# Splitting the value weights of time mixing on GpSimd in the stage before

## What is computed

```python
xn = _layernorm(x, ln_w, ln_b)
prev = jnp.pad(xn[:, :-1, :], ((0, 0), (1, 0), (0, 0)))
xk = xn * tmk + prev * (1.0 - tmk)        # the same for xv (tmv) and xr (tmr)
k = jnp.einsum('btd,ed->bte', xk, Wk)
v = jnp.einsum('btd,ed->bte', xv, Wv)
r = jax.nn.sigmoid(jnp.einsum('btd,ed->bte', xr, Wr))
decay = jax.nn.sigmoid(decay_w)
# over time t: S = decay * S + k_t * v_t, kept for each t as S_seq
out = x + r * jnp.einsum('btd,ed->bte', S_seq, Wo)
```

## Time and profile before

| | us |
|---|---|
| median of 3 runs | 2179.92 |
| lowest and highest | 2178.80, 2180.19 |
| the profiled execution: its time | 2187.31 |
| the profiled execution: its span | 2185.3 |
| busy in the span: TensorE | 2126.6 |
| ScalarE | 1399.6 |
| VectorE | 1391.0 |
| GpSimd | 304.9 |
| the two stages meet at about | 1936 |
| time mixing ends at about | 1994 |

### The profile page before, as it was taken

The page is one execution under the profiler, slowest core; times in us unless marked ns, Lnnn a source line. Parts: engine busy times, 40 slices in busy tenths (PEclk is TensorE's granted clock), DMA queues, the critical chain, the costliest instruction groups (busy, mean ns, idle before and its releaser), DMA issues. The chain is left out here.

```text
span 2185.3 us, 38691 instructions
## 1 busy us (share of the span) xinstructions
PE 2126.6 (97%) x15099; PEld 1654.0 (76%) x15099; DVE 1391.0 (64%) x2369; ACT 1399.6 (64%) x2701; POOL 304.9 (14%) x277
## 2 busy tenths in 40 slices
PE   8999999999999999899999999999999999998998
PEld 6787777787775567688888857777787778777775
DVE  6555455455565753699999974554554554587887
ACT  3666566666655544788888845665666666557774
POOL 1221212112110000200000211211122121103001
PEclk9999999999999999999999999999999999999999
DMA  4001001010104102799999930101000010013996
GB/s 164 20 21 40 21 21 40 21 40 21 34 26 151 36 4 100 307 368 375 356 350 360 364 124 7 39 21 40 21 36 24 21 40 20 21 59 136 362 357 234
DMA packets 53796, 262.10 MB, mean 120 GB/s; under 512 B 9576, under 2 KB 9960, under 8 KB 26992
## 3 DMA queue, kind: packets, MB, share of 16 engines
q1 hardware_dynamic: 47312, 244.42, 30.2%
q0 software_dynamic: 2560, 8.39, 1.1%
q10 hardware_dynamic: 3744, 6.82, 0.8%
HBM read 243.61 MB, written 15.99 MB: 119 GB/s over the span
## 5 line engine op out<-in xcount | busy, mean ns | idle before, releaser
L645 DVE COPY c_pt<-bank 128x512 f32<-128x512 f32 x256 | 177.2, 692 | 560.8 <-PE bank L443 560.7
L863 ACT ACTIVATE c_pr<-wide,c_nmax 128x512 f32<-128x512 f32 x512 | 348.8, 697 | 120.0 <-DVE c_nmax L637 62.1
L443 PE MATMUL bank<-ident,c_pr 128*128 128x128 f32 x2048 | 266.0, 273 | 1.0 <-ACT c_pt L870 0.7
L443 PEld LDWEIGHTS bank<-ident,c_pr 128*128 128x128 f32 x2048 | 238.2, 140 | 37.5 <-DVE c_pt L645 2.1
L841 ACT ACTIVATE c_khi<-bank,c_cols 128x512 fp32r<-128x512 f32 x128 | 87.9, 687 | 252.3 <-PE bank L95 252.3
L870 ACT COPY c_pt<-bank 128x512 f32<-128x512 f32 x256 | 150.4, 587 | 62.0 <-PE bank L443 61.8
L637 DVE CUSTOM_DVE_ANT_0 wide<-wide,land 128x512 f32<-128x512 f32 x256 | 169.2, 723 | 1.9 <-PE wide L427 1.7
L640 DVE TENSOR_REDUCE c_nmax<-wide 128x1 f32<-128x512 f32 x256 | 158.9, 683 | 1.8 <-PE wide L427 1.7
L312 POOL TENSOR_TENSOR c_clo<-land,c_chi 128x512 fp32r<-128x512 f32 x64 | 82.1, 1288 | 510.5 <-ACT c_chi L827 510.5
L459 PEld LDWEIGHTS bank<-c_pt,c_v 128*32 128x32 f32 x4096 | 104.1, 109 | 49.6 <-issue 47.1
L459 PE MATMUL bank<-c_pt,c_v 128*32 128x128 f32 x4096 | 138.4, 276 | 1.5 <-issue 1.4
(11 more groups left out here) (473 smaller groups left out, 5079.8 us busy)
## 6 DMA issues: line engine op xcount, KB each, us to landing
moe_hr<-in_L_ffn_w SPq DMA_DIRECT2D x68, 1024.0 KB, 7.8
land<-in_L_ffn_w SPq DMA_DIRECT2D x34, 1024.0 KB, 8.2
land<-in_ctx SPq DMA_DIRECT2D x31, 1024.0 KB, 4.9
moe_raw<-in_L_ffn_w SPq DMA_DIRECT2D x18, 1024.0 KB, 7.4
moe_raw<-in_L_ffn_we_gate SPq DMA_DIRECT2D x8, 1024.0 KB, 7.8
land<-in_L_ffn_we_up SPq DMA_DIRECT2D x8, 1024.0 KB, 6.9
moe_raw<-in_L_ffn_we_down SPq DMA_DIRECT2D x8, 1024.0 KB, 8.0
moe_raw<-in_L_ffn_we_up SPq DMA_DIRECT2D x7, 1024.0 KB, 7.2
```

Of the source, the lines that this page charges most:

```text
L443: last = pe.transpose(TB[n % 2][:, h * P:(h + 1) * P], pr[:, u % 2, h, n * P:(n + 1) * P], k["ident"][:])
L645: nc.vector.tensor_copy(pt[:, n, :], TB[0][:]).then_inc(pt_dve, 1)
L863: nc.scalar.activation(pr[:, u % 2, h, :], S[h][:], ACT.Exp, bias=nmax[:, b % 2, i, at:at + 1], scale=-1.0 if masked else 1.0, accum_out=d ...
```

## The change

The split of the value weights moves out of time mixing. In the second attention GpSimd, behind its last instruction, waits until Wv has landed and until the last value product of the attention is done, copies Wv (128x2048) into the first half of `home_hi`, and subtracts the two into the first half of `home_lo`. ScalarE and VectorE no longer do this at the start of time mixing, and the counts of the waits on `wlo` and `whi` go down by one; the loads of Wk and Wr are both issued at once, the one of Wo as before when the key weights are split. The six column loads go into the second attention, behind the loads of gamma and beta, into a tile of their own that outlives the stage. The decay's sigmoid moves on ScalarE from ahead of zT to behind the high part of the key weights, and GpSimd's copy into `rate`, which waits for it, with it.

```diff
+        next_split = sem("next_split")
@@ stage_cross, SyncE
                     sp.dma_start(beta_row, t[L + "beta"].partition_broadcast(P)).then_inc(row_in, 16)
+                    for i, n in enumerate(("ln_w", "ln_b", "tmk", "tmv", "tmr", "decay_w")):
+                        sp.dma_start(k["mix"][:, i, :], t["L1_attn_" + n]).then_inc(k["mix_in"], 16)
@@ stage_cross, GpSimd
                 nc.gpsimd.tensor_tensor(mine[:, 0:D // 2], mine[:, 0:D // 2], new[:, 0:D // 2], ALU.add).then_inc(early_joined, 1)
+                if norm:
+                    pool.wait_ge(k["landed"][0], 16 * (landings[0] + 1))
+                    pool.wait_ge(v_made, T4 * G - 1)
+                    nc.gpsimd.tensor_copy(wv_hi, k["land"][0][:]).then_inc(next_split, 1)
+                    pool.wait_ge(next_split, 1)
+                    nc.gpsimd.tensor_tensor(wv_lo, k["land"][0][:], f32(wv_hi), ALU.subtract).then_inc(next_split, 1)
@@ stage_rwkv
-        cols = m.sb("cols", [P, 6, C])
+        cols = k["mix"]
@@ SyncE
-                for i, n in enumerate(names):
-                    sp.dma_start(cols[:, i, :], t["L1_attn_" + n]).then_inc(s_["c_in"], 16)
                 sp.dma_start(raw[1], weights[1]).then_inc(w_in[1], 16)
                 for i in (2, 3):
-                    sp.wait_ge(s_["wlo"], i - 1)
+                    after(sp, s_["wlo"], i - 2)
                     sp.dma_start(raw[i % 2], weights[i]).then_inc(w_in[i], 16)
@@ TensorE
-                    pe.wait_ge(s_["wlo"], i + 1)
+                    after(pe, s_["wlo"], i)
-                pe.wait_ge(s_["wlo"], 3)
+                pe.wait_ge(s_["wlo"], 2)
-                pe.wait_ge(s_["wlo"], 4)
+                pe.wait_ge(s_["wlo"], 3)
@@ ScalarE
                 nc.scalar.sqrt(std[:], ve[:]).then_inc(s_["std"], 1)
-                high_weights(0)
-                act.wait_ge(s_["c_in"], 16 * len(names))
-                nc.scalar.activation(decay[:], cols[:, 5, :], ACT.Sigmoid).then_inc(s_["decay"], 1)
+                act.wait_ge(k["mix_in"], 16 * 6)
                 act.wait_ge(s_["rate"], 1)
@@
                 high_weights(1)
+                nc.scalar.activation(decay[:], cols[:, 5, :], ACT.Sigmoid).then_inc(s_["decay"], 1)
@@ VectorE
-                    dve.wait_ge(s_["whi"], i + 1)
+                    dve.wait_ge(s_["whi"], i)
@@
-                low_weights(0)
-                dve.wait_ge(s_["c_in"], 16 * len(names))
+                dve.wait_ge(k["mix_in"], 16 * 6)
@@ build
+            "mix": ctx.enter_context(nc.sbuf_tensor("mix", [P, 6, C], F32)),
+            "mix_in": nc.alloc_semaphore("mix_in"),
```

More of the change, by code:

```diff
@@ L2328, in stage_rwkv @@
         raw = [tile[:].rearrange("p (c n) -> p c n", c=C) for tile in k["land"]]
-        landings = list(k["landings"])
         grow, shift = m.sb("grow", [P, NB]), m.sb("shift", [P, NB])
@@ L2340, in stage_rwkv @@
         state, shi, slo, r = rise, hi[0], lo[0], zn
-        names = ("ln_w", "ln_b", "tmk", "tmv", "tmr", "decay_w")
         mix_col = (3, 2, 4)
-        s_ = {n: m.sem(n) for n in ("c_in", "dstep", "std", "zn", "turned", "zT", "decay", "rise", "blend", "hi", "lo",
+        s_ = {n: m.sem(n) for n in ("dstep", "std", "zn", "turned", "zT", "decay", "rise", "blend", "hi", "lo",
                                     "whi", "wlo", "v_made", "vT", "k_made", "kv", "state", "shi", "slo", "r_made", "r", "o_made",
@@ L2421, in high_weights @@
                 def high_weights(i):
[L2422 to L2425, removed]
+                    act.wait_ge(w_in[i], 16)
                     nc.scalar.copy(whi[i], raw[i % 2]).then_inc(s_["whi"], 1)
```

## The result

| | before | changed |
|---|---|---|
| median in the same set, 15 runs each | 2184.18 | 2191.09 |
| lowest and highest | 2178.80, 2189.01 | 2184.99, 2198.59 |
| profiled execution: span | 2185.3 | 2190.2 |

The ratio is 1.0031 with a 95% interval of 1.0022 to 1.0040: the change makes the kernel 4.8 to 8.7 us slower. The median of before, 2179.92 over three runs, is 2184.18 over fifteen.

A forecast was written before the change was run, and what follows sets the result against it. The VectorE and ScalarE chain from zT was taken to set time mixing's length, VectorE the attention's end. + 2.83 - 1.40 + 0.34 + 1.3 = + 3.1 on the median 2179.92 gave 2183.0; range 2178.6 to 2185.2.

The forecast's parts named there:

- The tail: End of the second cross attention: VectorE's two-input instructions wait for GpSimd's copy and subtraction, 2.83 later.
- rival B: Attention's tail: GpSimd is slow, copy 3.7 and subtraction 5.1, delay 5.2; sum + 5.1, 2185.0; chance 0.12.
- the rise: First rise in time mixing (L2497, 0.75): ended 0.55 after a GpSimd copy, taken as showing that copies hold VectorE.
- Rival C: Attention's tail: VectorE isn't held over such long instructions, only the gain is left; - 1.1, 2178.9; chance 0.12.
- The front: Start of time mixing: zT starts at about 1939.0 in place of 1940.38, 1.40 gained, at least 1.0.
- rival D: Front of time mixing: zT still starts late, for columns or transposes, so no gain; + 4.5, 2184.4; chance 0.06.
- The six column loads: SyncE's queue in the attention: six at under 0.5 fit in a pause of 15 and cost nothing.
- the decay's table load: ScalarE, behind the second weights in time mixing: 1.28 for the table, hidden in 3.02 of idle time.
- The copy of the decay: GpSimd in time mixing: the rate copy waits for VectorE and holds the next blend; 0.34 lost, between 0 and 0.46.
- The clock at the meeting: TensorE between the stages: a gap of 2.5 likely drops the clock; 1.3 lost, between 0.8 and 1.7.
- rival A: Meeting of the stages: the clock stays up in the gap; + 1.8, 2181.7; chance 0.20.
- The gap ahead of the third product: TensorE in time mixing: the first product's slow stretch goes, giving 1.5 where TensorE wasn't the bound; counted as nothing.

The follow-up runs named there:

- best: Changed kernel, split ahead of GpSimd's last three instructions, decay's copy later, 10 constant matmuls ahead of the third product; 0.9998 and 0.9997 against the kernel before.
- tail_only: Kernel before plus only GpSimd's copy and subtraction in the attention's tail, time mixing still splitting the weights itself; ratio 1.0010.
- again2: The changed kernel without any edit, measured in a third set; ratio 1.0023 against the kernel before.
- tail_memset: Kernel before plus four GpSimd memsets of 128x2048 in the attention's tail; one execution, 2180.57, against a median of 2183.82 for the kernel before.
- third: Changed kernel plus 18 matmuls on constants on TensorE between the key product and the third product; ratio 1.0017 against the kernel before.

## Why the prediction was wrong

**The range.** 2178.6 to 2185.2 against a median of 2191.09. I added the sum to 2179.92, a median of three runs that lie within 1.4 of each other. Fifteen runs spread over 10 and have their median at 2184.18. The range took in the bounds of the terms, but nothing for where the kernel itself would be measured. Even with the right sum, plus 5.5, I would have named 2185.4, already outside it. The forecast of plus 3.1 stood against plus 6.9 in that set and 5.5 over three. So of the 8.1 between 2183.0 and 2191.09, 4.3 is where the kernel before itself came to lie, and 3.8 is the change: the step that failed, below, is 1.6 of it, and the rest is open.

**The tail: right.** Predicted: L668 0.65 late, the subtraction of the mean ending 0.55 after GpSimd, 2.83 in all. Measured: 0.61, 0.54, and a tail longer by 2.68. GpSimd's copy took 1.89 (1.9 predicted), the subtraction 4.54 (4.6). The 4.50 of the Trainium skill (GPSIMD Engine Reference, section Elementwise — side-by-side cycle accounting) is for an addition of this size; the subtraction comes within 0.04 of it. Taking the 0.92 of the decay's copy as in part waiting was the choice that kept rival B out. `best` confirms the direction and not the size: alone the copy takes 0.61, so 0.31 of the 0.92 was waiting and not 0.46. Of the three rows that showed VectorE held, the rise was a weak one: it took 0.75, and 0.69 with no copy beside it. That a copy holds VectorE is shown now, by L677 (0.90 against 0.29). Rival C is out by `tail_only`, B by the two times.

**The front: right.** 1.40 predicted, at least 1.0; 1.16 to 1.22 measured where the clock stays up, which puts rival D out. The six column loads on SyncE's queue and the decay's table load cost nothing that shows: with the copy moved away in `best`, the middle is as long as before's.

**The copy of the decay: right.** 0.34 predicted; the two blends (L2479) take 1.76 in place of 1.41, and the middle is 0.38 longer (28.89 against 28.51). Without the collision the 0.35 is gone (28.53).

**The clock at the meeting: right.** A gap of 2.5 predicted, 2.77 found; 1.3 for the slow stretch. Front 2.96 with the clock up and 4.07 to 4.96 with it down: 1.1 to 2.0, of which the 2.0 lies outside the 0.8 to 1.7 of the prediction. `again2` is rival A's case. That the clock fell in the other two profiles of the changed kernel was given as likelier than not, and the ground for it, the one fall behind 2.05, was thin.

**The gap ahead of the third product: the step that failed.** The prediction says: "the slow stretch of before goes; that gives TensorE 1.5 where it was not the bound, so nothing." The first half is right: the gap ahead of the first product is 0.75 and the clock stays up there. The key product then ends 0.72 sooner behind zT than before, and the third product starts 0.38 later, so TensorE waits for the last low part for 2.08 in place of 0.99. But that time is not nothing. In the three profiles of the changed kernel the clock falls 0.7 to 1.5 behind the end of this gap, and the slow stretch that had been in the first product, where it was hidden, is now in the third, where it sets the end: 1.6 (26.83 against 25.24). With this term and the measured sizes the first profile's sum is + 2.7 - 1.2 + 0.35 + 1.4 + 1.6 = + 4.85; less the 0.3 of idle time noted under the table and 0.1 at the meeting itself this is the 4.5 measured (77.32 - 72.80). I had used the very row that would have warned me, the 0.50 behind 2.05 idle, for one gap, and not asked which other gap of that size the change would open.

The loss belongs to the clock staying up in the first product, more than to the change itself: `tail_memset`, whose time mixing is that of before, had it too. In all nine profiles of the changed kernel and its variants the clock was up in the first product. How much of the 1.6 stands between the medians of the two kernels is therefore not known.

**What stays open.** The three profiles of the changed kernel are 4.5, 4.2 and 3.1 longer in the stretch; the timed runs say 5.5, give or take 1.3. The sum of the parts lies at the lower edge. If the executions of before often have the clock down in their own third product, as `tail_memset` had, the parts should come to less still. By the means (3.9 against 5.5), 1.6 of the loss, give or take 1.3 and perhaps more, has no cause shown. Nothing outside the stretch differs in a steady way between the profiles, but what follows it varies by 6.5 from one profile to the next, so a small steady cost there could not be seen.

## What to carry to other kernels

GpSimd is free only when the work beside it on VectorE doesn't need what it needs. Before filling its idle time, go through VectorE's instructions in that time and look for those with two inputs in SBUF; move GpSimd's reading work to where there are none, even if GpSimd has to be idle later instead. Cutting it into four pieces didn't help here. A microsecond taken from an engine that isn't the bound need not be worth nothing: here it turned into idle time of TensorE, and the slow clock behind that landed in the part that is the bound.

## What the hardware showed

- GpSimd waits for VectorE as VectorE waits for GpSimd. The copy of the decay was issued at 1956.56 into a VectorE subtraction that ended at 1957.30, and ended 0.47 later: 1.21 in all, against 0.61 with nothing in its way.
- With a gap of 2.07 to 2.08 ahead of the third product the clock fell in six profiles of seven, 0.7 to 1.5 behind the gap's end; with 2.75 to 2.93 at the meeting in five of six, between 0.7 ahead of the gap's end and 0.6 behind it. The gap's length alone doesn't decide.
- After such a fall the granted clock was 0.50 for 3.4, also while TensorE was busy throughout (x9 matmuls in the row of 1974.10), and in one profile, `third`, for 6.8.
- The same kernel's executions spread over 10 us and more, while its parts, where the clock is the same, repeat to a few hundredths from profile to profile (the tail 16.77 to 16.79, the end 25.22 to 25.25). For changes of a few us the profile's parts are the better measure.
